# Head mixing on one core: score sums ahead of the projection, the addition to x one tile later, and a scaling moved between a product and its sum

## The reference

```python
Q = (x @ Wq.T).reshape(b, s, h, hd)      # h = 16 heads, hd = 8
K = (x @ Wk.T).reshape(b, s, h, hd)
V = (x @ Wv.T).reshape(b, s, h, hd)
scores = jnp.einsum('bshd,bstd->bsht', Q, K) / math.sqrt(hd)   # 16 x 16 for each token
attn = jax.nn.softmax(scores, axis=-1)
out = jnp.einsum('bsht,bstd->bshd', attn, V).reshape(b, s, dm)
return out @ Wfc.T
...
x = x + _L0_attn_ref(_layernorm(x, axis=-1), ...)
x = x + 0.5 * _L0_ffn_ref(_layernorm(x, axis=-1), L0_ffn_router_w, ...)   # experts, top 2 of 8
```

## Time and profile before

| | |
|---|---|
| median of 3 runs | 2918.82 us (2918.11 to 2923.93) |
| the profiled execution, its own time | 2907.47 us |
| its span | 2905.7 us |
| mean granted clock of TensorE | 0.912 |
| busy in the span: PE, DVE, ACT, POOL | 79%, 70%, 50%, 32% |
| head mixing, 325 to 650 us of the span: busy PE, DVE, ACT, POOL | 261.79, 241.47, 50.91, 134.67 us |
| granted clock in these 325 us | 0.86 |

### The profile page before, as it was taken

One profiled execution on the slowest core, in us unless ns is written; L12 is line 12 of the kernel. 1 busy time (PEld: TensorE's weight loads), 2 busy tenths in 40 slices (PEclk: granted clock), 3 DMA queues, 4 the chain that ended last, 5 costly groups with the idle time before them and its releaser, 6 DMA issues. The chain is left out here.

```text
span 2905.7 us, 45477 instructions
## 1 busy us (share of the span) xinstructions
PE 2297.3 (79%) x13880; PEld 1435.4 (49%) x13880; DVE 2042.8 (70%) x5186; ACT 1455.4 (50%) x3123; POOL 925.2 (32%) x978
## 2 busy tenths in 40 slices
PE   3399588857967699989999997757958598778887
PEld 3398477647955222222222222547947597533334
DVE  4466688756654699999999992555658565579994
ACT  2266311115644458888888786225643365533332
POOL 4644234444431400010110100364435544323330
PEclk9999799878989879999999998978979699889998
DMA  4122200002220310000000000012220122200001
GB/s 155 46 64 62 58 8 15 11 21 56 66 79 15 123 61 20 18 18 20 18 18 18 18 10 31 19 34 57 64 78 29 48 64 78 62 0 0 1 0 29
DMA packets 111195, 115.76 MB, mean 40 GB/s; under 512 B 21904, under 2 KB 94192, under 8 KB 110192
## 3 DMA queue, kind: packets, MB, share of 16 engines
q1 hardware_dynamic: 92512, 76.38, 9.0%
q0 software_dynamic: 17408, 35.95, 3.7%
q10 hardware_dynamic: 1040, 0.53, 0.1%
HBM read 67.55 MB, written 44.83 MB: 39 GB/s over the span
## 5 line engine op out<-in xcount | busy, mean ns | idle before, releaser
L1878 DVE TENSOR_REDUCE attn_mx<-bank 128x1 f32<-128x512 f32 x1024 | 641.4, 683 | 63.2 <-PE bank L1657 55.2
L1779 ACT ACTIVATE attn_pT<-bank 128x512 f32<-128x512 f32 x1024 | 539.9, 603 | 128.1 <-PE bank L1672 127.5
L1657 PE MATMUL bank<-attn_K,attn_Q 48*128 48x512 bf16 x1024 | 338.4, 399 | 49.6 <-DVE attn_mx L1878 28.4
L1672 PE MATMUL bank<-attn_Q,attn_K 51*128 51x512 bf16 x1024 | 332.9, 389 | 2.5 <-ACT attn_pT L1779 1.6
L1685 PE MATMUL bank<-attn_pT,attn_vb 128*32 128x512 f32 x2048 | 277.5, 613 | 20.1 <-ACT attn_pT L1779 12.1
L1838 POOL TENSOR_TENSOR attn_m_rem<-attn_m_rem,attn_m_parts 8x128 f32<-8x128 f32 x128 | 53.5, 418 | 680.7 <-ACT attn_m_parts L1792 680.7
L1657 PEld LDWEIGHTS bank<-attn_K,attn_Q 48*128 48x128 bf16 x1024 | 72.0, 94 | 377.0 <-DVE attn_mx L1878 326.0
L2634 POOL TENSOR_TENSOR mix_rS<-mix_rT,mix_S 128x512 f32<-128x512 f32 x64 | 80.2, 1254 | 185.1 <-DVE mix_S L2693 91.7
L1004 PE MATMUL bank<-mix_prod_qk,ident 128*128 128x256 f32 x512 | 121.7, 393 | 0.0
L1004 PEld LDWEIGHTS bank<-mix_prod_qk,ident 128*128 128x128 f32 x512 | 101.4, 200 | 24.8 <-issue 11.2
L1064 ACT ACTIVATE mix_kv<-bank 128x256 f32<-128x256 f32 x32 | 12.2, 380 | 180.3 <-PE bank L997 164.3
(11 more groups left out here) (617 smaller groups left out, 5862.3 us busy)
## 6 DMA issues: line engine op xcount, KB each, us to landing
w<-in_L_w SPq DMA_DIRECT2D x4, 2048.0 KB
ffn0a_x_ring<-xs_rows SPq DMA_DIRECT2D x72, 65.0 KB, 1.8
ffn0b_x_ring<-xs_rows SPq DMA_DIRECT2D x72, 65.0 KB
ffn2a_x_ring<-xs_rows SPq DMA_DIRECT2D x72, 65.0 KB, 1.8
ffn2b_x_ring<-xs_rows SPq DMA_DIRECT2D x72, 65.0 KB, 1.8
ffn0a_y_back<-y_rows SPq DMA_DIRECT2D x8, 512.0 KB, 3.8
ffn1a_in_y_back<-y_rows SPq DMA_DIRECT2D x8, 512.0 KB
ffn2a_y_back<-y_rows SPq DMA_DIRECT2D x8, 512.0 KB
```

The lines of the kernel that those rows point to most:

```text
L1657: nc.tensor.matmul(a_bank[n % 3][:], slot(net.Q, h, 0, KROWS)[:, qt * P:(qt + 1) * P], slot(net.K, h, 0, KROWS)[:, hf * CH:(hf + 1) * CH], ...
L1672: nc.tensor.matmul(s_bank[n % 3][:], slot(net.K, h, 0, KROWS + MROWS)[:, kt * P:(kt + 1) * P], slot(net.Q, h, 0, KROWS + MROWS)[:, hf * CH ...
L1779: nc.scalar.activation(pT[:, kt % RING, hf * CH:(hf + 1) * CH], s_bank[(n * HPB + hf) % 3][:], ACT.Exp, scale=HD ** -0.5).then_inc(exp_rea ...
L1878: nc.vector.tensor_reduce(mx[:, h % 2, qt, hf:hf + 1], a_bank[n % 3][:], AX.X, ALU.max).then_inc(a_used, 1)
```

## The change

TensorE sums the scores of tile n + 2 ahead of the projection where i = 0. VectorE's addition to x and the moments go from the end of the iteration i = 0 to the middle of i = 1, behind `times_keys`. The scaling of a GpSimd tile goes from ahead of `share` of the next tile to between that tile's product and its sum; for that `times_values` is cut in two. ScalarE's `exp` of a GpSimd tile waits for an earlier count of `mixed`. No instruction is added or taken away.

```diff
@@ tensor
                 if n + 4 < NTT:
                     qkv(n + 4)
+                if 0 <= n + 2 < NTT:
+                    sum_scores(n + 2)
                 if after == 0:
                     project(c - 1)
-                if 0 <= n + 2 < NTT:
-                    sum_scores(n + 2)
@@ scalar
             def exp(n):
                 if is_summed(n):
                     need(act, pv_done, summed_before(n) - 1)
-                need(act, mixed, n - 1)
+                    need(act, mixed, n - TPC + 1)
+                else:
+                    need(act, mixed, n - 1)
                 act.wait_ge(logit_ready, n + 1)
@@ vector
                 chain.then(nc.vector.tensor_tensor(own_pv[:]...  ALU.mult))
+
+            def sum_values(n):
                 chain.wait()
                 chain.then(nc.vector.tensor_reduce(m_bank[n % 2][:, 0:D], own_pv[:]...  AX.X, ALU.add))
@@ vector, the loop
                     times_keys(n + 3)
-                if n > 0 and is_summed(n - 1):
+                if after == 1:
+                    add(c - 1)
+                    norm.stats(dve, c - 1)
+                if n >= 0:
+                    share(n)
+                if n >= 0 and not is_summed(n):
+                    times_values(n)
                     dve.wait_ge(sum_ready, summed_before(n - 1) + 1)
                     scale(n - 1)
-                if n >= 0:
-                    share(n)
-                    if not is_summed(n):
-                        times_values(n)
-                        scale(n)
-                if after == 0:
-                    add(c - 1)
-                    norm.stats(dve, c - 1)
+                    sum_values(n)
+                    scale(n)
```

## The result

The changed kernel took 2890.14 us in the median of four runs (2880.59 to 2892.90), the kernel before 2918.85 us. The ratio is 0.9892, with a 95% interval of 0.9867 to 0.9917: 1.1% faster. 2902 us (a ratio of 0.9942) had been forecast, with 2889 to 2919 as the range; 0.9892 of 2918.85 is 2887 us. The direction was right and the gain larger than the forecast: the median of 2890.14 us lies at the lower end of the range, the 2887 us that the ratio gives lie just outside it. The profiled execution took 2889.47 us, its span was 2887.7 us.

A forecast was written before the change was run, and what follows sets the result against it. No engine full; a loop between VectorE and TensorE bounds the stage. 11.4 - 15.5 + 3.4 + 7.2 + 2.2 + 2.9 = 11.6 us, plus 5 for clock, makes 17: 2918.8 to 2902 us, range 2889 to 2919.

The forecast's parts named there:

- Scores ahead of the projection: TensorE sums scores before projecting, so VectorE's maximum of the third tile starts earlier; 11.4 us gained over seven rounds.
- M to S: VectorE: end of a round's last scaling (M) to start of the i=2 tile's maximum (S); about 8.3 us mean.
- Addition and moments: On VectorE, moved behind the keys' product, they come onto the path; 2.21 us lost per round, 15.5 us in all.
- S to M: VectorE: start of the i=2 tile's maximum (S) to the end of the next last scaling (M); about 28.5 us.
- The waits at the scalings: VectorE's scalings, now between product and sum, no longer wait for value sums; gains of 3.4, 7.2, 2.2 and 2.9 us.
- The clock: TensorE from M to S keeps full clock more often; between nothing and 18.6 us, taken as 5 us.
- the wait for the scores: VectorE's maximum waiting for score sums; a sign, to grow from 18.8 to some 32 us.
- exp costed at nothing: ScalarE's exp of a GpSimd tile: the changed count keeps it from becoming late, no cost.
- The second wait: Rival: the fourth tile's scaling wait moves with the scaling or returns elsewhere; 2917 us, no change; chance 0.22.
- The low clock: Rival: TensorE's low clock lasts beyond S, delaying value sums and scaling; slower, 2931 us; chance 0.12.
- Full clock throughout: Rival: TensorE keeps full clock from M to S in all rounds; 30 us gained, 2889 us; chance 0.14.

The follow-up runs named there:

- e9_scores_scale: The changed kernel with the addition and moments put back to the end of i = 0; ratio 0.9912 to the kernel before.
- e11_turn_last: The changed kernel with the projection to q, k, v and the score sums of i = 0 ahead of the turn; 2877.13 us against 2922.34, ratio 0.9843.
- e18_after_fourth: The changed kernel, unchanged, run again on a chip where the kernel before took 2920.44 us; ratio 0.9875.
- e10_old_exp_wait: The changed kernel with exp of a GpSimd tile waiting for the scaling of the tile before, as before the change; ratio 0.9953 to the kernel before.

## Why the prediction was right and where it failed

*Scores ahead of the projection, 11.4 us.* Right: 5.05 us from M to S at full clock in three rounds, 5.2 forecast. In round 7, which has no projection to q, k, v, it is 4.19, 1 us better than I had it.

*Addition and moments, a loss of 2.21 us each.* Right. S to M stays at 28.8 although the waits of 0.49 and 1.5 us are gone from it, and in e9_scores_scale, with the addition back, it is 27.2. With both of these terms and the next one, the forecast had the sum of the seven stretches from S to M 0.2 us shorter; it is 1.4 us shorter (198.1 to 196.7). So what exceeds the forecast lies between M and S.

*The waits at the scalings, 15.7 us.* Right for the first comparison's chip, where they are gone. On a chip without late semaphores the five waits of 1.5 us do not exist, so there 7.2 us of the term fall away (S to M 27.1 before, 28.8 after).

*The clock, "I take 5 us, as if one or two of six rounds kept it, since the idle time doesn't vanish".* This is the step that failed for the first comparison. M to S of rounds 2 to 7 fell by 3.87 us each (9.84 to 5.97), of which 1.55 were the moved scores; the rest, 6 x 2.3 = 14 us, is clock and the 1 us of round 7, where I had 5. The bounds of 0 to 18.6 us were right; the value within them was not. Three rounds kept the clock, not one or two. They are those in which the idle time ahead of the turn fell to 1.2 us; in the other three it stayed at 2.8 to 2.9 and the clock was low. For the same reason the wait for the scores is 19.8 us and not 32, which was worked out with 8.3 us from M to S. I had seen that the 1.5 us of the late semaphore lie in this idle time. What I missed is that they decide it: without them the idle time is short after long value sums, with them it is long in every round, 26.1 us in all in the first trace of the kernel before, 15.7 in its second. With the lateness taken away by the split scatters, on another chip that has it, M to S is 8.1 us where the first trace had 9.8, and the kernel gained 0.7% with nothing else changed. The changed kernel hides the lateness behind a share and a value product, so that its stage takes 234 to 238 us on every chip (four traces), while that of the kernel before takes 244 and 248 without lateness and 264 with it (one trace). On chips without lateness M to S falls by 2.3 and 3.0 us, the scores' 1.55 and 0.75 to 1.4 of clock, together 4.5 to 8.5 us: there the 5 us were about the right size, and the ratios (0.9953, 0.9951) have the forecast (0.9942) within their intervals. That agreement is in part luck, since 7.2 of the forecast's 17 us were waits that these chips don't have.

*exp costed at nothing.* Right as forecast, with the changed count; without it 14 us would be lost.

*The rivals.* The second wait did not stay in either case: it was held by the scatters' issue and not by the scaling, so it was a fixed end, as I had taken it. The low clock never lasted beyond S. Full clock throughout (2889 us) came near as a time, but three of six rounds still had low clock.

Open is why TensorE's semaphores are late beside GpSimd's scatters on some chips. A kernel that leaves out all scatters, or puts other work of GpSimd in their place, was not tried.

## What to carry to other kernels

A wait to which the profile gives an unlikely releaser is a reason for a second trace before its length goes into a sum: here it went with the chip, and it drew a lower clock behind it. Two moves that gain nothing alone (scores ahead, addition later) brought 0.4% together, because each alone only moved the wait to another place in VectorE's order; so a chain is best cut at the engine that closes it, and whatever can be done before the closing instruction is put ahead of it, as in e11_turn_last.

## What the runs showed of the hardware

The same program took 2897 to 2900 us in three of the comparisons, each on a chip of its own, and 2919 to 2922 in the other three. In traces of the slower ones, TensorE's semaphore increments for matmuls that run beside GpSimd's indirect scatters came up to 3.9 us after the matmuls' recorded end (e18_after_fourth, round 2), and 2.4 to 2.6 us after the start of the last scatter issue; with four of the eight scatters issued elsewhere, so that the last one came 5 to 7 us ahead of the matmuls' end, they were on time. TensorE's clock was at 1.2 GHz for part of the turn and what follows it in all 35 rounds with 2.3 to 4.3 us of idle time ahead of the turn, and in six of 61 with 1.6 us or less; once matmuls of 2.2 us filled the idle time it stayed at 2.4 GHz in that place. A VectorE instruction of 0.16 us that came while GpSimd's product of 4.06 us ran took 2.15 us and ended with the product, in six rounds of six (e10_old_exp_wait); the scaling and the sum just ahead of it, beside the same product, kept their length of 0.29 and 2.29 us.
